# Taps accumulated in PSUM, a projection one step later, four row buffers, and another order of the work behind the attention, in a perceiver block on one core

## What is computed

```python
x = x + xattn(ctx, layernorm(x))   # 8 batches, 16 heads of 64, 1024 + 64 keys; then @ Wo
x = x + mamba(layernorm(x))        # in_proj 256 -> 2*512; causal conv of 4 taps; silu; x_proj; softplus; scan
x = x + moe(layernorm(x))          # 8 experts, 512 picked tokens each, gelu; scatter-add

# inside mamba, per token pair-tile (128 tokens = 2 sequences of 64)
xc = sum(x_pad[:, k:k + L] * conv_w[:, k] for k in range(4)) + conv_b; xc = silu(xc)
dt = softplus(dbc[0] * dt_w + dt_b)            # dbc = xc @ x_proj_w, 33 rows: dt, 16 B, 16 C
h = exp(dt * A) * h + dt * B * xc; y = sum_n h * C + xc * D; y = y * silu(z); y @ W_out
```

## Time and profile before

| | us |
|---|---|
| median of three runs | 858.48 |
| lowest and highest | 856.98, 860.85 |
| the profiled execution | 856.04 |
| its span | 854.3 |
| span of the steps (first to last start of line 914) | 42.8 to 644.0 |
| TensorE, VectorE, ScalarE, GpSimd busy | 746.7, 521.2, 417.7, 413.5 |

### The profile page before, as it was taken

One profiled execution on the slowest core, in us unless ns is written; L12 is line 12 of the kernel. 1 busy time (PEld: TensorE's weight loads), 2 busy tenths in 40 slices (PEclk: granted clock), 3 DMA queues, 4 the chain that ended last, 5 costly groups with the idle time before them and its releaser, 6 DMA issues.

```text
span 854.3 us, 14283 instructions
## 1 busy us (share of the span) xinstructions
PE 746.7 (87%) x5379; PEld 683.0 (80%) x5379; DVE 521.2 (61%) x1094; ACT 417.7 (49%) x1122; POOL 413.5 (48%) x374
## 2 busy tenths in 40 slices
PE   5979999999999999997979999979898541879996
PEld 3579999999999999997879899869897430548895
DVE  5265475565766777889774688885675493760112
ACT  2435454543555565554654665536564253634341
POOL 2818017003601896686366956762767675700000
PEclk9999999999999999998998999989999765989998
DMA  9540100010011003001110120000011128101720
GB/s 316 227 110 2 62 14 1 6 63 8 2 62 32 9 13 89 19 19 50 28 31 13 27 75 17 15 7 10 19 27 26 19 93 305 60 0 64 246 86 28
DMA packets 48840, 49.07 MB, mean 57 GB/s; under 512 B 18356, under 2 KB 43648, under 8 KB 47616
## 3 DMA queue, kind: packets, MB, share of 16 engines
q1 hardware_dynamic: 48768, 48.11, 18.3%
HBM read 43.71 MB, written 4.26 MB: 56 GB/s over the span
## 4 chain that ended last, share of the span: by engine, by line
PE 59%; DVE 15%; POOL 9%; issue 7%; DMA 5%; ACT 4%; SPq 1%; POOLq 0%; DVEq 0%; ACTq 0%
PE psum L1536 18%; PE psum L1569 13%; PE psum L1552 4%; PE psum L1913 3%; PE psum L1903 3%; PE psum L1509 3%; POOL work L606 2%; POOL work L599 2%; DVE work L900 2%; DVE conv L876 2%; POOL y_sum L612 2%; PE psum L1489 2%; DVE rowmax L914 2%; PE psum L1591 2%; DVE pt_lo L824 2%
## 5 line engine op out<-in xcount | busy, mean ns | idle before, releaser
L1209 ACT ACTIVATE pt_hi<-psum 128x512 fp32r<-128x512 f32 (+1 forms) x192 | 87.3, 490 | 214.5 <-PE psum L1552 164.6
L1569 PE MATMUL psum<-kvn_hi,pt_hi 128*128 128x256 f32 x512 | 150.4, 294 | 2.4 <-DVE pt_hi L821 2.4
L1569 PE MATMUL psum<-kvn_hi,pt_lo 128*128 128x256 f32 x512 | 145.0, 283 | 0.0
L1569 PE MATMUL psum<-kvn_lo,pt_hi 128*128 128x256 f32 x512 | 144.9, 283 | 0.0
L914 DVE TENSOR_REDUCE rowmax<-psum 128x1 f32<-128x728 f32 x64 | 58.6, 915 | 97.1 <-PE psum L1536 96.9
L606 POOL TENSOR_TENSOR work<-work,bc 128x512 f32<-128x512 f32 x48 | 66.9, 1395 | 89.7 <-DVE work L900 89.7
L1569 PEld LDWEIGHTS psum<-kvn_hi,pt_hi 128*128 128x128 f32 x512 | 98.0, 191 | 2.7 <-DVE pt_hi L821 2.6
L1536 PE MATMUL psum<-kvt_hi,qk_hi 128*128 128x364 f32 (+1 forms) x384 | 93.2, 352 | 6.7 <-ACT prob L1329 4.3
L1569 PEld LDWEIGHTS psum<-kvn_lo,pt_hi 128*128 128x128 f32 x512 | 98.0, 191 | 0.1
L1569 PEld LDWEIGHTS psum<-kvn_hi,pt_lo 128*128 128x128 f32 x512 | 97.8, 191 | 0.0
L1536 PE MATMUL psum<-kvt_lo,qk_hi 128*128 128x364 f32 (+1 forms) x384 | 86.8, 336 | 0.0
(11 more groups left out here) (233 smaller groups left out, 1582.5 us busy)
## 6 DMA issues: line engine op xcount, KB each, us to landing
w<-in_L_ffn_W_dram SPq DMA_DIRECT2D x16, 1024.0 KB, 8.0
ctx_nat<-in_ctx_dram SPq DMA_DIRECT2D x8, 1024.0 KB, 5.2
bc<-dbc_keep SPq DMA_DIRECT2D x48, 128.0 KB, 4.7
q_keep<-q_t SPq DMA_DIRECT2D x1, 2048.0 KB, 8.4
q_cur<-q_keep SPq DMA_DIRECT2D x14, 128.0 KB, 3.2
wk_nat<-in_L_xattn_Wkv_dram SPq DMA_DIRECT2D x1, 1024.0 KB, 6.1
wq_sb<-in_L_xattn_Wq_dram SPq DMA_DIRECT2D x1, 1024.0 KB, 11.8
wv<-in_L_xattn_Wkv_dram SPq DMA_DIRECT2D x1, 1024.0 KB, 14.0
```

The costliest lines, as they stand in the source:

```text
L1209: act.activation(pt_hi[u][:, t0:t1, :], where[:, 0:(t1 - t0) * P].rearrange("p (t m) -> p t m", m=P), ACT.Copy)\
L1569: pe.matmul(PV, w[u][:, j, :], x_[slot][:, j, :], start=(j == 0 and w is pt_hi and x_ is kvn_hi), stop=False)
```

## The change

- In the steps, taps 0 to 2 of the convolution write to bank TP[1] in PSUM and read their running sum from there; the last tap reads PSUM and writes `conv` in SBUF. The tiles are done two and two, in steps r = 2 and r = 3; r = 4 has none. TensorE waits for them before it transposes into TP[1] in the step after each.
- The projection of a finished pair moves from r = 24 to r = 25, `mixed` from r = 25 to r = 26; the first then waits for side job 2 in place of 0.
- ROWS is 4 in place of 3.
- Behind the attention the normalised tile is made and taken in ahead of the lists, `onehot` stands ahead of the first left unit, the taps are all VectorE's, sixteen of them read from the projection's own PSUM bank, shifted on the output side, tap by tap over the four tiles; they stand behind the counts. `xpad` isn't used there and ScalarE's copy and taps go. `picks(0)` stands ahead of the step sizes, `list_slots` ahead of x_proj, ScalarE's decays of the third left unit ahead of the silu. Expert 0 is loaded with experts 1 to 3, behind `b_all`.

```diff
-    ROWS = 3
+    ROWS = 4
@@ sync
             sp.dma_start(b2_sb[:], b2).then_inc(ld_b2, 16)
-            load_expert(0, 0)
...
-            for i in range(1, RING):
+            for i in range(RING):
                 load_expert(i, i)
@@ vector, taps(t, tiles)
-                        o = conv[:, d, :].rearrange("p (s l) -> p s l", l=L)
+                        part = TP[1][:, d * P:(d + 1) * P].rearrange("p (s l) -> p s l", l=L)
                         if k == 0:
-                            ins = dve.tensor_scalar(o, xpad[:, d, :, 0:L], convw[:, d, 0:1], dvec[:, 0, d:d + 1],
+                            ins = dve.tensor_scalar(part, xpad[:, d, :, 0:L], convw[:, d, 0:1], dvec[:, 0, d:d + 1],
                                                     ALU.mult, ALU.add)
                         else:
                             dve.wait_ge(v_tap, made + len(tiles) * (k - 1) + j + 1)
+                            o = part if k < TAPS - 1 else conv[:, d, :].rearrange("p (s l) -> p s l", l=L)
                             ins = dve.scalar_tensor_tensor(out=o, in0=xpad[:, d, :, k:k + L],
-                                                           scalar=convw[:, d, k:k + 1], in1=o, op0=ALU.mult,
+                                                           scalar=convw[:, d, k:k + 1], in1=part, op0=ALU.mult,
                                                            op1=ALU.add)
@@ vector, step
-                t = pair_at(g, 25)
+                t = pair_at(g, 26)
                 if t is not None:
                     mixed(t, MB[:, 0:C])
...
-                for r, tiles in ((2, (0,)), (3, (1, 2)), (4, (3,))):
+                for r, tiles in ((2, (0, 1)), (3, (2, 3))):
@@ vector, behind the attention
             token_stats(last_)
+            dve.wait_ge(v_rs, 2 * last_ + 1)
+            dve.tensor_scalar(xn[:], x1[:, last_, :], tmv[:, 0:1], trs[:, 0:1], ALU.subtract, ALU.mult).then_inc(v_xn, 1)
...
             dve.tensor_copy(tile_f[:], index[:, 2, :]).then_inc(r_idx, 1)
-            dve.wait_ge(v_rs, 2 * last_ + 1)
-            dve.tensor_scalar(xn[:], x1[:, last_, :], tmv[:, 0:1], trs[:, 0:1], ALU.subtract, ALU.mult).then_inc(v_xn, 1)
+            dve.wait_ge(v_xt, INLINE + 1)
+            dve.wait_ge(v_z, INLINE)
+            dve.tensor_scalar(xn_t[:, 0, :], psum[:, 0, 0:P], nwb[:, 0, 0:1], nwb[:, 1, 0:1], ALU.mult, ALU.add)\
+                .then_inc(v_xte, 1)
             dve.wait_ge(r_tab, 1)
...
-            token_scale(last_)
-            scan_unit(left[0])
             dve.tensor_tensor(onehot[:], iota_f[:].unsqueeze(1).to_broadcast((P, SC * E, P)),
                               place_f[:].unsqueeze(2).to_broadcast((P, SC * E, P)), ALU.is_equal).then_inc(r_oh, 1)
-
-            for d in range(DT):
-                dve.wait_ge(m_tap, d + 1)
-                o = conv[:, d, :].rearrange("p (s l) -> p s l", l=L)
-                for k in range(1, TAPS):
-                    ins = dve.scalar_tensor_tensor(out=o, in0=xpad[:, d, :, k:k + L], scalar=convw[:, d, k:k + 1],
-                                                   in1=o, op0=ALU.mult, op1=ALU.add)
-                    if k < TAPS - 1:
-                        link(ins)
-                ins.then_inc(m_conv, 1)
+            scan_unit(left[0])
+            token_scale(last_)
             scan_unit(left[1])
...
             dve.tensor_tensor(coef[:], counts, comb[:], ALU.mult).then_inc(r_val, 1)
+
+            dve.wait_ge(v_xz, INLINE + 1)
+            dve.wait_ge(v_dts, INLINE)
+            for k in reversed(range(TAPS)):
+                late = TAPS - 1 - k
+                for d in range(DT):
+                    x_in = psum[:, YB, d * P:(d + 1) * P].rearrange("p (s l) -> p s l", l=L)[:, :, 0:L - late]
+                    o = conv[:, d, :].rearrange("p (s l) -> p s l", l=L)[:, :, late:]
+                    if late == 0:
+                        ins = dve.tensor_scalar(o, x_in, convw[:, d, k:k + 1], dvec[:, 0, d:d + 1], ALU.mult, ALU.add)
+                    else:
+                        dve.wait_ge(m_tap, DT * (late - 1) + d + 1)
+                        ins = dve.scalar_tensor_tensor(out=o, in0=x_in, scalar=convw[:, d, k:k + 1], in1=o,
+                                                       op0=ALU.mult, op1=ALU.add)
+                    ins.then_inc(m_tap, 1)
...
             dve.tensor_copy(most_i[:], most[:]).then_inc(r_pos, 1)
+            dve.wait_ge(r_pos, 2)
+            picks(0)
...
             scan_unit(left[2])
-            dve.wait_ge(r_pos, 2)
-            picks(0)
@@ scalar, behind the attention
-            act.wait_ge(v_xz, INLINE + 1)
-            act.wait_ge(v_tap, DT * TAPS * INLINE)
-            act.activation(xpad[:, :, :, TAPS - 1:], psum[:, YB, :].rearrange("p (d s l) -> p d s l", s=BP, l=L),
-                           ACT.Copy).then_inc(v_pad, 1)
-            act.wait_ge(v_pad, INLINE + 1)
-            act.wait_ge(v_dts, INLINE)
-            for d in range(DT):
-                act.activation(conv[:, d, :].rearrange("p (s l) -> p s l", l=L), xpad[:, d, :, 0:L], ACT.Identity,
-                               scale=convw[:, d, 0:1], bias=dvec[:, 0, d:d + 1]).then_inc(m_tap, 1)
             decays(left[1])
+            decays(left[2])
...
-            decays(left[2])
@@ tensor
+                for r in (3, 4):
+                    t = pair_at(g, r)
+                    if t is not None:
+                        pe.wait_ge(v_tap, TAPS * (DT * t + 2 * r - 4))
...
-                t = pair_at(g, 24)
+                t = pair_at(g, 25)
                 if t is not None and t < INLINE - 1:
                     pe.wait_ge(v_y, t + 1)
-                    pe.wait_ge(s_mlo, misc_count(b + 1, 0) if b + 1 < B else MISC * B)
+                    pe.wait_ge(s_mlo, misc_count(b + 1, 2) if b + 1 < B else MISC * B)
                     w_out(zs[t % 2], MB[:, 0:C]).then_inc(v_yo, 1)
...
+            list_slots()
             pe.wait_ge(v_xc, INLINE + DT)
             x_proj(psum[:, DB[0], :]).then_inc(v_dbc, 1)
-            list_slots()
```

More of the change, by code:

```diff
@@ L269, in perceiver_kernel @@
         ld_bc = [sem(f"ld_bc{i}") for i in range(ROWS)]
-        m_pad, m_tap, m_conv, m_dt0, m_dta, m_dec, m_drv, m_scan, m_c, m_rd, m_acc, m_zs, m_out = (sem("m_" + n) for n in (
-            "pad tap conv dt0 dta dec drv scan c rd acc zs out").split())
+        m_pad, m_tap, m_dt0, m_dta, m_dec, m_drv, m_scan, m_c, m_rd, m_acc, m_zs, m_out = (sem("m_" + n) for n in (
+            "pad tap dt0 dta dec drv scan c rd acc zs out").split())
         r_idx, r_tab, r_oh, r_cnt, r_val, r_pre, r_pos, r_b1, r_b1e = (sem("r_" + n) for n in (
@@ L1379, in _ @@
             for d in range(DT):
-                act.wait_ge(m_conv, d + 1)
+                act.wait_ge(m_tap, DT * (TAPS - 1) + d + 1)
                 act.activation(xc[:, d, :], conv[:, d, :], ACT.Silu).then_inc(v_xc, 1)
@@ L1835, in _ @@
             pe.wait_ge(v_y0, INLINE + 1)
-            pe.wait_ge(v_pad, INLINE + 1)
+            pe.wait_ge(m_tap, DT * TAPS)
             pe.matmul(psum[:, YB, :], ident[:], y_skip[:].rearrange("p d m -> p (d m)"), start=True, stop=False)
```

4 lines of the change are left out of this document (removed).

## The result

| | before | changed |
|---|---|---|
| median, us | 859.66 | 829.74 |
| lowest and highest | 856.98, 861.89 | 829.13, 832.14 |
| the profiled execution, its span | 856.04, 854.3 | 829.16, 827.4 |
| line 914, step 21 to step 63 | 421.66 | 405.19 |
| start of step 63 to the first state scan | 72.88 | 61.40 |

What follows compares the result with a forecast made beforehand. TensorE's stream bounds the kernel, held in places by other engines; behind the attention, orders and landings decide. -12.7 - 4.6 - 3.3 - 8.2 = -28.8 from 856.04 gives 827.2, 829.7 on the median's scale; forecast 829, range 815 to 842.

Steps and rivals of the forecast that it cites:

- Taps, -12.7: Convolution taps in steps 21 to 55: running sums in PSUM avoid GpSimd's hold; 1.4 - 5.9 - 5.9 - 2.3 = -12.7 us.
- Price of a tap: VectorE tap through PSUM: 0.06 us added, 0.34 from start to start, 2.7 for eight; bounds 0.28 and 0.44.
- Rival A: Taps with running sum in PSUM still wait for GpSimd; taps +5, kernel 848 (850 on the median's scale); chance 0.06.
- B: Rival: taps in PSUM are dear, so slower; loses from 0.79 us a tap, 888 at 1.3; chance 0.04.
- Pair 0, +1.4: Steps 21 and 22: eight taps in place of four, +0.9, then PSUM's price, +0.5; together +1.4 us.
- so it isn't paid twice: Pair 0's taps: TensorE's new wait costs nothing beyond the +1.4, since line 914 is late by the same time.
- Projection in steps 43 and 44, -4.6: Projection one step later: step 45 starts at 459.8, now 464.36; -7 without job 2's wait, -2.6 with the clock down.
- Projection in steps 59 to 62, -3.3: Projection one step later: step 61 comes 4.4 us sooner, -3.3 left after mixed waits; bounds -2 and -5.
- Four buffers, 0: Fourth row buffer: 0 in the steps; behind the attention it lets SP pass the last units' rows sooner.
- Behind the attention, -8.2: Up to the first state scan: earlier dbc store without expert 0 ahead, b_all sooner; -8.2 us, bounds -11 and -5.
- Rival C: GpSimd and the clock keep more: half of the projection's and the last item's gain gone, 837; chance 0.16.
- rival D: More comes: half-clock stretches of TensorE go, the tail takes its bound; -40, so 818; chance 0.16.

Runs made afterwards that it cites:

- experiments 1 to 4: Changed kernel, taps varied: in SBUF, two tiles and two, TensorE's wait kept, 855.14 us; old lists in PSUM, 829.42; then experiment 3, experiment 4.
- experiment 4: Changed kernel with its new tap lists (two tiles and two), taps in SBUF, without TensorE's waits for them: 848.92 us.
- experiment 10: Kernel before with only expert 0's loads moved behind the store of dbc and the loads of b_all: 850.11 us, 0.989 of before.
- experiment 3: Changed kernel with taps wholly as before: in SBUF, tiles (0), (1, 2), (3) over three steps, no TensorE wait for them: 846.42 us.
- experiment 8: Changed kernel with the projection early in steps 44 and 60, not behind the low part, and mixed ahead of the scan: 823.13 us, 0.9607 of before.
- experiment 6: Changed kernel with the projection back at steps 43 and 59, mixed one step sooner, the wait for side job 0 again: 832.70 us.
- experiment 5: Changed kernel with three row buffers in place of four: 829.59 us.
- experiments 10 and 11: Besides experiment 10, the second is the changed kernel with expert 0 loaded ahead of the store of dbc again: 835.11 us.
- experiment 12: Changed kernel with pick put back behind the left unit, ahead of the step sizes, as in the kernel before: 831.95 us.

## Why the prediction was right, and where not

**The time is right to 0.7 us on the medians, in part by luck: errors stand against each other twice.** The sum gave 827.2 for the profiled execution, which took 829.2, 2.0 more; but the 2.4 us by which the median of before lay above its profiled execution are 0.6 after. And inside the sum the projection fell short by 3.6 where the tail brought 3.3 more.

- *Taps, -12.7: measured -12.4, and shown to be the place.* "An instruction with one input in PSUM doesn't" wait for GpSimd: right, by experiments 1 to 4. Price of a tap: I took 0.34 from start to start and got 2.26 / 8 = 0.28, the lower bound. Behind the first tap its length is 0.344 to 0.352 (0.340 to 0.344 where it writes SBUF) against 0.337 in SBUF, and eight in turn take 2.26 us where eight unheld ones in SBUF take 2.17 (experiment 4, step 21), so the 0.06 that I added for PSUM is 0.01. Rival A is refuted; B too, a tap being far from 0.79.
  The Trainium skill (VectorE: DVE Perf Modes, The TRN2 errata) would have a tap with a source in PSUM 62 cycles dearer; here the difference is 3 to 15 ns, so for this operation, with its other input in SBUF, the measurement decides against it. Its section Why PSUM operands drop a tier would have the first taps dearer by 0.07, and the trace agrees: all twelve took 403 to 408 ns into PSUM, where the shortest in the kernel before, into SBUF, took 338.
- *Pair 0, +1.4: right number, wrong cause.* The step that failed is "so it isn't paid twice". I charged VectorE's longer list and took TensorE's wait as covered by it. It is the other way about: the list costs nothing (28.86 against 28.85), the wait costs 1.4. The same wait is likely the +0.8 of step 39, which I had at 0 (step 23, where it stands alone, is 0.8 longer as well); no run shows it apart in step 39, and the cheaper taps paid for it in the sum.
- *Step 39 of before, 10.21, wasn't a firm base.* In experiment 10, the same work there takes 12.79. These are TensorE's rows and the stretch of its projection, first of before, then of that experiment:

```profile
400.43 0.33 PE L1544 MATMUL psum<-ident,prob 128*128 128x128 f32 x1 [0.51 <-DVE pt_lo L824]
...
403.32 2.05 PE L1619 MATMUL psum<-xn_t,win 128*128 128x128 f32 x16 [1.26 <-DVE kvt_lo L782]
```

```profile
403.30:405.40 2.10, 2.08 (x18) 2.08 (x19) 2.03 (x3) 0.55 (x2) 2.02 (x3) 1.00 0.00 0
```

```profile
400.60 0.33 PE L1543 MATMUL psum<-ident,prob 128*128 128x128 f32 x1 [1.96 <-DVE pt_lo L823]
...
403.49 3.78 PE L1618 MATMUL psum<-xn_t,win 128*128 128x128 f32 x16 [1.26 <-DVE kvt_lo L781]
```

```profile
403.30:405.40 2.10, 1.91 (x9) 1.92 (x10) 2.00 (x4) 0.71 (x3) 2.02 (x2) 0.50 0.00 0
```

  One pause is longer by 1.45 us, and the clock of the projection is 0.50 in place of 1.00. So what PSUM saves in steps 37 to 39 is 5.9 against one trace of before and 7.9 against experiment 3.
- *Projection in steps 43 and 44, -4.6: measured -1.0, outside the bound of -2.6.* Found as a pause, mis-sized in two terms. "Scan 1.2" was 2.20, since that scan lies beside two GpSimd instructions (+1.0). "Projection 1.8 at full clock, logits 3.1" was 7.2 from the end of the low part to line 914, for the clock is at 0.50 behind the pause (+2.3), which is 4.24 long and not 2.4. The bound took in the clock and not the scan. The two steps took 25.3 in experiment 10, with nothing in them changed, so against that trace the move brings nothing. And TensorE had no need to pause: what held it was the bank it shares with the low part, by experiment 8.
- *Projection in steps 59 to 62, -3.3: measured -3.1, half of it the clock.* With the move undone (experiment 6) only 1.5 come back. The other 1.6 are the half clock that the eight matmuls had in the trace of before (3.68 us against 1.99 behind the same pause of 2.54). The sum took that trace's clock as given, so its -3.3 is right for this trace and twice what the move was worth in experiment 6.
- *Four buffers, 0: measured 0*, by experiment 5, and nothing in the tail either.
- *Behind the attention, -8.2: measured -11.5, its bound was -11.* Mechanism right: SP's queue, by experiments 10 and 11. Mis-sized, by one small term after another: the store, 3 us, took 1.3, and `b_all`, 8.3, took 8.8 or less (679.49 to 688.26, with no wait left to see). The convolution ends 47.2 behind the start of step 63, where I had 48.7 and before has 47.5: sixteen taps take 4.4 us, 0.28 each, not 0.32. So `dtx_l` ends at 59.0, not 62.0, and the drive starts at 60.0, not 63.3.
- Rival C (GpSimd and the clock keep more) came true in steps 43 and 44, rival D in the tail, and they cancel to 0.3 us.

## What to carry to other kernels

A wait is worth what its end sets off, not its length: taking away 21 us in which TensorE stood for taps gave back 4, while taking a wait of 4.2 us out of one step gave 5.8, about 2 of them by the clock. When a wait protects a bank, ask who reads the result: the 5.8 us came from moving one piece of work ahead of the slow reader of its bank. A small store on which a chain hangs goes ahead of bulk loads in its queue, and running sums on VectorE beside a busy GpSimd go to PSUM. Before a step of one trace is taken as the base of a sum, look at the clock in it: the same code in the same place took 10.2 or 12.8 us here.

## What the runs showed of the hardware that was not expected

- A tap that reads and writes PSUM, with its other input in SBUF, takes 344 to 352 ns for 128 x 128. The same tap in SBUF takes 337 ns when GpSimd is idle and up to 1384 (in experiment 4 up to 2065) when it isn't.
- A first tap, whose only tensor input is in SBUF, takes 403 to 408 ns into PSUM and is never held; into SBUF it takes 338 ns at the least and up to 1324 beside GpSimd.
- A scan of 512 elements from SBUF took 2.20 us beside GpSimd's instructions, where the median of the 48 is 1.22.
- The hold goes both ways. `pick` began while GpSimd's product `y_skip` ran and took 5.06 us in place of 4.40 (experiment 12); the GpSimd product that began while `pick` ran took 5.45 in place of 1.27.
- TensorE's granted clock was 1.00 behind a pause of 1.5 us and 0.50 behind one of 4.2. Behind one of 2.54 us it was 1.00 in experiment 6 and 0.54 in the kernel before. It was 0.50 behind three pauses in a row of 1.96, 0.85 and 1.26, where 0.51, 0.85 and 1.26 left it at 1.00.
- A store of 16.5 KB landed after 1.3 us alone and after 3.9 close behind the load of a unit's rows. Behind the two weight loads of 1 MB each it landed 6.7 and 10.1 us after its own issue, which is 12.0 and 11.1 after that of the first weight load.
